# Attention, batch order and routing: a key copy, a product and six operations issued at other places

## The chip, the core and the metric

The kernel runs on one core of one Trainium2 chip. The metric is the device time in microseconds from start to end of one execution; lower is better. The core has five engines with a queue of their own each, and every queue runs strictly in the order in which the program issues: TensorE (PE) multiplies into the PSUM banks, VectorE (DVE) and ScalarE (ACT) read those banks and SBUF, GpSimd (POOL) reads SBUF only, SyncE (SP) issues the loads. Engines wait for each other by semaphores only: an instruction that waits holds up everything behind it on its engine.

## What is computed

Cross attention over 8 batches of 112 tokens, then a feed-forward layer with 8 routed experts (the two best for each token) and a shared one, everything in fp32:

```python
x = x + _L0_xattn_ref(_layernorm(x, axis=-1), ctx_512, L0_xattn_Wq, L0_xattn_Wkv_expand, L0_xattn_Wout)
x = x + _L0_ffn_ref(_layernorm(x, axis=-1), ...)
# attention: 16 heads of 32, causal mask
qp = q @ Wq.T; k, v = jnp.split(latent_kv @ Wkv_expand.T, 2, axis=-1)
out = softmax(mask(qh @ kh.T / sqrt(32))) @ vh          # per head
return out @ Wout.T
# feed-forward
scores = jax.nn.softmax(x @ gate_weight.T, axis=-1)
topk_w, topk_idx = jax.lax.top_k(scores, 2)
act = silu(gu[..., :F]) * gu[..., F:]                   # per expert, F = 352
y = jnp.einsum('tef,te,ehf->th', act, combine, down_weights)
sact = silu(sgu[:, :Fs]) * sgu[:, Fs:]                  # shared expert, Fs = 704
y = y + sact @ shared_down.T
```

## The kernel before

The 896 tokens are 8 batches of 112 rows for the attention and 7 tiles of 128 rows for the rest. Every fp32 operand of a large product is split into a high and a low part ("_hi", made by ScalarE, and "_lo", made by VectorE as the difference), and a product is three passes over the pairs lo-hi, hi-lo, hi-hi. There is no planner: the order on each engine is written out by hand in one block for each engine, and the batches are pipelined across engines.

**Attention, loop over b = 0 to 7.** In iteration b TensorE computes the scores of batch b+1 (`scores`), transposes the four groups r of batch b's probabilities (`transposed(b, r)`), computes the output projection of the batch tile b-2 (`out_proj(b - 2, ...)`, twelve passes into bank D, split 9 and 3 around the last two transposes), transposes tile b-3 of the next layer's input (`t2`), projects the values of batch b+1 (`v_proj`) and multiplies probabilities with values into bank CC (called O(b) here). The key and query projections of the second half of the batches are spread over iterations 0 and 1; the last one, `k_proj(1, 3, CC)`, goes through the same bank CC, so that O(1) has to wait (semaphore KT) until its result is copied out. VectorE does that copy (`put_kT(3)`, helper line L1351) behind `inverse(2, 0)`, `masked(2, 3)`, `inverse(2, 1)`. `inverse(b, r)` takes reciprocals of the row sums and waits for ScalarE's exponentials `exps(b, r)` (L1038); `masked(b, r)` adds the mask and finds the maximum; `put_v` and `oT_lo` follow. GpSimd multiplies the probabilities with the reciprocals (`normalised`, L430) and does the statistics' last step and the normalisation of the next layer (`apply2`). ScalarE copies the transposed probabilities out (`put_pT`, probT) except group 1 of batches 2 and later, which VectorE copies (L1333), and makes `put_x2T` and `put_oT`. From iteration 2 on ScalarE does `put_x2T(b - 3)` before the copies `put_pT(b, 2)` and `put_pT(b, 3)`. `add_attention(n)` (L1298) adds bank D to the residual and takes the statistics.

**Shared stage.** The shared expert's 704 columns are worked off in slices j = 0 to 5; in each, `shared_gu(j, t)` computes gate and up for the token blocks t = 0 (4 tiles) and t = 1 (3 tiles), ScalarE and VectorE make the activation (`shared_silu`, `shared_mul`, L1474, `shared_hi`, `shared_lo`), and `shared_down(j, t)` multiplies with the down weights into four banks, from which VectorE adds into the residual (`add_shared`, L1494). Amid this VectorE does the routing: a chain of small dependent operations, 56 elements wide, each waiting for the one before (`link`): softmax, `pick` (the best expert), `pick` (the second), the sums picked and before, then (semaphore trip) TensorE's rank products (L846 to L849), copies of their result (L1551, L1552) and the slots. GpSimd then scatters the rows to the experts' tiles in memory. In TensorE's order: shared_down(0,0), shared_gu(1,1), shared_down(0,1), shared_gu(2,0), the rank products, shared_down(1,0). `shared_down(0, 1)` waits for the additions of `add_shared(0, 0)` (semaphore sres), since it uses the same banks; `shared_gu(2, 0)` waits for `shared_mul(1, 0)` (sact).

**Expert loop.** 21 tiles of 128 gathered rows, each with its expert's weights split on the fly.

The lines of TensorE's helper `product` are L554, of the transposes L615 (probabilities) and L546 (rows), of the scores L626, of O(b) L763; L993 is ScalarE's helper for the high parts and copies, L1279 VectorE's for the low parts.

Of the kernel before, what the change touches and what calls it, by code (L numbers as in the profile page):

```python
# [43 lines left out]
def build(nc, x, ctxT, wqT, wkvT, woT, gateT, guT, dnT, sguT, sdnT, out):  # L44
# [220 lines left out]
    with nc.Block() as block:  # L265
# [275 lines left out]
        def _(pe):  # L541
# [165 lines left out]
            for b in range(NB):  # L707
# [28 lines left out]
                if b >= 2:  # L736
                    pe.wait_ge(s["QT"], C * NBLK)
                    if b >= 3:
                        pe.wait_ge(s["x1"], b - 2)
                    if b == 2:  # L740
                        pe.wait_ge(s["wo_hi"], C)
                        pe.wait_ge(s["wo_lo"], C)
                    out_proj(b - 2, 0, 9)
                transposed(b, 2)
# [3 lines left out]
                if b >= 2:  # L748
                    out_proj(b - 2, 9, 3 * C)
                if b + 1 < NB:  # L750
# [240 lines left out]
        def _(act):  # L991
# [27 lines left out]
            def put_x2T(n, bank_):  # L1019
                act.wait_ge(s["T2"], n + 1)  # L1020
                hi(x2T[0][:, :, n * P:(n + 1) * P], as_chunks(bank_, P), "x2T_hi")
# [76 lines left out]
            for b in range(NB):  # L1098
# [12 lines left out]
                if b + 1 < NB:  # L1111
                    exps(b + 1, 1)
                if b >= 3:
                    put_x2T(b - 3, CC)
                if b >= 2:
                    put_pT(b, 2)
                    put_pT(b, 3)
# [146 lines left out]
        def _(dve):  # L1264
# [84 lines left out]
            def put_kT(j):  # L1349
                dve.wait_ge(s["K"], C + j + 1)  # L1350
                dve.tensor_copy(kT[1][:, j, :], CC[:, 0:W]).then_inc(s["KT"], 1)  # L1351
# [73 lines left out]
            masked(1, 2)  # L1425
            for b in range(NB):
                if b + 1 < NB:
                    inverse(b + 1, 0)
# [13 lines left out]
                if b >= 2:  # L1442
                    add_attention(b - 2)
                if b == 1:
                    put_kT(3)
                if b + 1 < NB:
# [61 lines left out]
            def pick(p, top, first, oh):  # L1508
# [23 lines left out]

            pick(prb, weight, first1, oh1)
            link(dve.scalar_tensor_tensor(out=prb2[:, :, :], in0=oh1[:, :, :], scalar=-2.0, in1=prb[:, :, :],
                                          op0=ALU.mult, op1=ALU.add))
            pick(prb2, second_w[:, :], first2, oh2)
            link(dve.tensor_tensor(picked[:, 0:NX, :], oh1[:, :, :], oh2[:, :, :], ALU.add))
            for n in range(NX):
# [3 lines left out]
            last.then_inc(s["trip"], 1)  # L1542
            add_shared(0, 0)
            shared_act(1, 0)
            add_shared(0, 1)
# [135 lines left out]
```

## Time and profile before

| | |
|---|---|
| time, median of 3 runs | 344.97 us (343.78 to 345.1) |
| profiled execution | 346.77 us, its span 345.0 us |
| TensorE busy | 327.2 us (95% of the span) |
| VectorE, ScalarE, GpSimd busy | 267.9, 233.1, 133.2 us (78%, 68%, 39%) |
| mean granted TensorE clock | 0.982 of full speed |
| stages in the span | attention to about 108 us, shared stage to about 196, expert loop to the end |

Times in views of the trace are microseconds from the start of the span. Busy TensorE time overstates how full it is, since matmuls are pipelined: one pass of 512 columns is listed with 0.39 us, but the next starts 0.23 us after it. The chain of work that ended last is followed back from the last instruction, at each step to what released it.

### The profile page before, as it was taken

The numbers are of one execution on the slowest core, as the hardware profiler recorded it, in microseconds if no ns is written. First come the engines' busy times: TensorE is split into PE (matmuls) and PEld (weight loads), VectorE is DVE, ScalarE is ACT, GpSimd is POOL, SyncE is SP. The second block draws the span as 40 slices with busy tenths as digits, with TensorE's granted clock in tenths as the row PEclk, the third lists the DMA queues.
The fourth block names the chain that finished last, engine by engine and source line by source line (L and its number), as shares of the span: only waits on it lengthen the run. The fifth ranks groups of instructions, "written<-read, shape, count | busy, mean of one in ns | idle before, by whom it ended". The sixth has DMA issues, their size and how long they took to land.

```text
span 345.0 us, 7024 instructions
## 1 busy us (share of the span) xinstructions
PE 327.2 (95%) x2285; PEld 281.6 (82%) x2285; DVE 267.9 (78%) x675; ACT 233.1 (68%) x582; POOL 133.2 (39%) x144
## 2 busy tenths in 40 slices
PE   7999979999999998999999899999999999999990
PEld 6898858777776786889898778889988998998980
DVE  4889757999936348855487999999998989999930
ACT  4666988999953232312326578898898889889830
POOL 4335464777844000164400007765742321231231
PEclk9999987999999999999999999999999999999996
DMA  7999300000002799994689953564455456455333
GB/s 232 378 341 379 110 1 3 3 2 1 3 2 95 289 357 327 430 327 152 217 253 236 299 179 82 96 135 101 84 117 130 84 89 138 103 89 120 71 42 50
DMA packets 31795, 53.01 MB, mean 154 GB/s; under 512 B 7440, under 2 KB 14992, under 8 KB 30736
## 3 DMA queue, kind: packets, MB, share of 16 engines
q1 hardware_dynamic: 27616, 43.34, 38.4%
q0 software_dynamic: 4144, 9.23, 14.9%
q8 instruction: 19, 0.31, 0.4%
q14 instruction: 16, 0.13, 0.1%
HBM read 32.22 MB, written 16.92 MB: 142 GB/s over the span
## 4 chain that ended last, share of the span: by engine, by line
PE 69%; ACT 10%; DVE 8%; DMA 6%; issue 3%; POOL 2%; POOLq 1%; SPq 0%; DVEq 0%; ACTq 0%
PE bank L554 26%; PE bank L877 21%; ACT prob L1038 5%; PE bank L901 5%; DMA out<-y_sb,dest 3%; PE bank L615 3%; PE bank L905 2%; PE bank L915 2%; PE bank L776 2%; PE bank L763 2%; PE bank L911 2%; DVE gu_parts L1279 2%; PE bank L546 2%; PE bank L626 1%; DMA w_sg<-sguT 1%
## 5 line engine op out<-in xcount | busy, mean ns | idle before, releaser
L533 POOL DMA_INDIRECT out<-y_sb,dest x21 | 38.4, 1830 | 114.9 <-DMA out<-y_sb,dest 68.1
L1279 DVE TENSOR_TENSOR gu_parts<-w_gu,gu_parts 128x704 fp32r<-128x704 f32 x84 | 77.0, 951 | 0.8 <-ACT gu_parts L993 0.4
L993 ACT ACTIVATE gu_parts<-w_gu 128x704 fp32r x84 | 66.2, 793 | 13.9 <-PE bank L877 12.3
L877 PE MATMUL bank<-gu_parts,xsT_hi 128*128 128x352 f32 x328 | 70.0, 335 | 1.4 <-DVE xsT_lo L1279 0.9
L877 PEld LDWEIGHTS bank<-gu_parts,xsT_hi 128*128 128x128 f32 x328 | 53.7, 188 | 8.8 <-issue 8.7
L877 PE MATMUL bank<-gu_parts,xsT_lo 128*128 128x352 f32 x164 | 39.7, 323 | 0.0
L554 PE MATMUL bank<-x2T_hi,w_sg_lo 128*128 128x512 f32 (+1 forms) x88 | 32.7, 372 | 0.2
L430 POOL TENSOR_TENSOR prob<-prob,rrow 112x448 f32<-112x448 f32 x30 | 27.5, 935 | 12.3 <-DVE rrow L1329 12.3
L554 PE MATMUL bank<-x2T_hi,w_sg_hi 128*128 128x512 f32 (+1 forms) x88 | 32.0, 363 | 0.0
L554 PE MATMUL bank<-x2T_lo,w_sg_hi 128*128 128x512 f32 (+1 forms) x88 | 31.9, 363 | 0.0
L506 POOL DMA_INDIRECT xs_dram<-x2n,slot_i x14 | 14.8, 1057 | 37.9 <-DVE eid L1574 33.9
L877 PEld LDWEIGHTS bank<-gu_parts,xsT_lo 128*128 128x128 f32 x164 | 28.7, 189 | 0.0
L993 ACT ACTIVATE act_s_hi<-act_s 128x512 fp32r<-128x512 f32 (+1 forms) x10 | 5.8, 577 | 32.5 <-DVE act_s L1474 18.9
L1279 DVE TENSOR_TENSOR dn_lo<-w_dn,dn_hi 128x1024 fp32r<-128x1024 f32 x21 | 25.6, 1217 | 2.6 <-ACT dn_hi L993 2.6
L1038 ACT ACTIVATE prob<-score,negmax 112x112 f32<-112x112 f32 x64 | 24.2, 405 | 0.0
L993 ACT ACTIVATE dn_hi<-w_dn 128x1024 fp32r x21 | 22.2, 1060 | 2.9 <-PE bank L905 2.9
L1038 ACT ACTIVATE prob<-bank,negmax 112x112 f32<-112x112 f32 x64 | 21.8, 374 | 2.5 <-DVE negmax L1323 2.5
L1494 DVE TENSOR_TENSOR xres<-xres,bank 128x512 f32<-128x512 f32 x35 | 22.3, 680 | 0.4 <-PE bank L807 0.4
L554 PEld LDWEIGHTS bank<-x2T_hi,w_sg_lo 128*128 128x128 f32 x88 | 16.5, 188 | 4.5 <-issue 2.2
L554 PEld LDWEIGHTS bank<-x2T_hi,w_sg_hi 128*128 128x128 f32 x88 | 16.5, 188 | 1.8
L554 PEld LDWEIGHTS bank<-x2T_lo,w_sg_hi 128*128 128x128 f32 x88 | 16.5, 188 | 1.7
L1279 DVE TENSOR_TENSOR w_sg_lo<-w_sg,w_sg_hi 128x1024 fp32r<-128x1024 f32 (+1 forms) x6 | 6.9, 1150 | 13.6 <-ACT w_sg_hi L993 13.6
(216 smaller groups left out, 830.8 us busy)
## 6 DMA issues: line engine op xcount, KB each, us to landing
w_gu<-guT SPq DMA_DIRECT2D x8, 1408.0 KB
xs_dram<-no_row SPq DMA_DIRECT2D x1, 5460.0 KB, 19.6
xs_in<-xs_dram SPq DMA_DIRECT2D x21, 256.0 KB, 4.5
w_dn<-dnT SPq DMA_DIRECT2D x8, 512.0 KB, 5.4
act_w<-act_e SPq DMA_DIRECT2D x19, 176.0 KB, 2.7
w_sg<-sguT SPq DMA_DIRECT2D x10, 256.0 KB, 5.4
w_dn<-dnT SPq DMA_DIRECT2D x8, 192.0 KB, 6.1
w_sd<-sdnT SPq DMA_DIRECT2D x5, 256.0 KB, 6.0
```

The lines of the kernel that those rows point to most:

```text
L430: pool.tensor_tensor(prob[r][:, :, :], prob[r][:, :, :], rrow[:, r, :].unsqueeze(2).to_broadcast([SQ, C, SQ]), ALU.mult)\
L506: pool.indirect_dma_start(out=xs_dram[:, :], out_offset=bass.IndirectOffsetOnAxis(ap=slot_i[:, k, n:n + 1], axis=0), in_=x2n[:, n, :], in_ ...
L533: pool.indirect_dma_start(out=out[:, :], out_offset=bass.IndirectOffsetOnAxis(ap=dest[:, i, 0:1], axis=0), in_=y_sb[i % 2][:, :], in_offse ...
L546: ins = pe.transpose(dst[:, c * P:(c + 1) * P], src[:, c * P:(c + 1) * P], ident[:, :])
L554: ins = pe.matmul(dst, a, b, start=start and n == 0, stop=stop and n == len(passes) - 1)
L615: ins = pe.transpose((A, B)[r % 2][0:SQ, c * SQ:(c + 1) * SQ], prob[r][:, c, :], ident[0:SQ, 0:SQ])
L877: ins = pe.matmul(dst[:, 0:F], xsT[x_][:, c, :], gu2[w_][:, c, f0:f0 + F], start=c == 0 and n == 0, stop=c == C - 1 and n == 2)
L901: pe.matmul(A[:, :], actT_split[0][:, k, :], dn2[part][:, k, :], start=k == 0 and part == 1, stop=False)
L993: act.activation(dst, src, ACT.Copy).then_inc(s[sem], 1)
L1038: ins = act.activation(prob[r][:, c, :], src, ACT.Exp, bias=negmax[:, r, c:c + 1], scale=-1.0, accum_out=rowsum[:, r, c:c + 1])
L1279: dve.tensor_tensor(lo_, src, hi_.bitcast(F32), ALU.subtract).then_inc(s[sem], 1)
L1494: dve.tensor_tensor(xres[:, n, :], xres[:, n, :], (B, CC, D, A)[i][:, :], ALU.add)\
```

## The change

- VectorE: `put_kT(3)` of iteration b = 1 moves from behind `inverse(2, 0)`, `masked(2, 3)`, `inverse(2, 1)` to the front of the iteration.
- TensorE, last iteration b = 7 only: `out_proj(5)` is split 6 and 6 passes instead of 9 and 3 around the transposes `transposed(7, 2)`, `t2(4)`, `transposed(7, 3)`.
- ScalarE, b = 7 only: `put_pT(7, 2)` goes before `put_x2T(4)`; for b = 2 to 6 the order stays as it was.
- VectorE, routing: the four additions `add_shared(0, 0)` and the product `shared_mul(1, 0)` go from behind the sums to behind the first `pick`, and `shared_lo(1, 0)` behind the second `pick` (`shared_act` is these two calls one after the other).

No instruction is added or removed.

```diff
@@ TensorE
+                    early = 9 if b + 1 < NB else 6
-                    out_proj(b - 2, 0, 9)
+                    out_proj(b - 2, 0, early)
                 transposed(b, 2)
                 if b >= 3:
                     t2(b - 3, CC)
                 transposed(b, 3)
                 if b >= 2:
-                    out_proj(b - 2, 9, 3 * C)
+                    out_proj(b - 2, early, 3 * C)
@@ ScalarE
+                if b == NB - 1:
+                    put_pT(b, 2)
                 if b >= 3:
                     put_x2T(b - 3, CC)
+                if 2 <= b < NB - 1:
+                    put_pT(b, 2)
                 if b >= 2:
-                    put_pT(b, 2)
                     put_pT(b, 3)
@@ VectorE, attention
             for b in range(NB):
+                if b == 1:
+                    put_kT(3)
                 if b + 1 < NB:
                     inverse(b + 1, 0)
...
                     add_attention(b - 2)
-                if b == 1:
-                    put_kT(3)
@@ VectorE, routing
             pick(prb, weight, first1, oh1)
+            add_shared(0, 0)
+            shared_mul(1, 0)
             link(dve.scalar_tensor_tensor(out=prb2[:, :, :], in0=oh1[:, :, :], scalar=-2.0, in1=prb[:, :, :],
                                           op0=ALU.mult, op1=ALU.add))
             pick(prb2, second_w[:, :], first2, oh2)
+            shared_lo(1, 0)
             link(dve.tensor_tensor(picked[:, 0:NX, :], oh1[:, :, :], oh2[:, :, :], ALU.add))
...
             last.then_inc(s["trip"], 1)
-            add_shared(0, 0)
-            shared_act(1, 0)
             add_shared(0, 1)
             shared_act(1, 1)
```

## Rows read from the trace of the kernel before

**Rows 1.** The chain that ended last, by engine (part 4 of the page).

```profile
PE 69%; ACT 10%; DVE 8%; DMA 6%; issue 3%; POOL 2%; POOLq 1%; SPq 0%; DVEq 0%; ACTq 0%
```

**Rows 2.** Pieces of that chain, batches 1, 2 and 4: start us, us, what.

```profile
49.33 0.18 DVE rrow L1329
49.51 0.52 DVE kT L1351
...
50.07 1.72 PE bank L763 x32
51.80 1.78 PE bank L626 x32
53.58 1.67 PE bank L615 x8
55.25 2.60 PE bank L554 x9
...
59.36 0.70 DVE xres L1298
...
68.18 0.90 PE bank L763 x32
69.08 0.98 PE bank L626 x32
70.06 0.94 PE bank L615 x8
71.00 2.10 PE bank L554 x9
...
76.21 0.95 PE bank L763 x32
```

**Rows 3.** Engine timelines, batches 1 and 2: start, us, instruction, [idle before <-releaser].

```profile
45.58 0.36 PE L554 MATMUL bank<-ctx_hi,w_kv_hi 128*128 128x448 f32 x1
...
47.75 0.40 PE L554 MATMUL bank<-w_kv_hi,ctx_hi 128*112 128x512 f32 x1
...
46.28 0.08 DVE L1323 DVE_READ_ACCUMULATOR2_ANT negmax<- 112x1 f32 x1
...
56.55 0.59 DVE L1333 COPY probT<-bank 112x448 f32<-112x448 f32 x1
...
51.86 0.54 ACT L1049 ACTIVATE oT_hi<-bank 128x448 fp32r<-128x448 f32 x1 [1.10 <-PE bank L763]
...
45.68 2.53 POOL L452 TENSOR_TENSOR w_o_lo<-w_o,w_o_hi 128x512 fp32r<-128x512 f32 x2
```

**Rows 4.** Busy time of the engines and granted clock (PEclk) in two stretches.

```profile
131.00:132.44 1.44, 0.38 (x3) 0.08 (x2) 1.34 (x6) 0.00 (x0) 0.00 (x0) 1.00 1.01 430
...
49.30:56.20 6.90, 6.13 (x75) 5.41 (x76) 4.58 (x29) 5.15 (x25) 2.80 (x3) 0.51 0.01 2
```

**Rows 5.** Timelines of TensorE and ScalarE before the last batch's product.

```profile
101.47 1.01 PE L763 MATMUL bank<-probT,v_sb 112*32 112x112 f32 x32 [0.47 <-issue]
...
100.43 0.97 ACT L993 ACTIVATE probT<-bank 112x448 f32<-112x448 f32 x2
```

**Rows 6.** Timelines of VectorE and TensorE around the routing, shared stage.

```profile
128.33 0.22 DVE L1514 TENSOR_TENSOR oh<-down,first 128x56 f32<-128x56 f32 x1
...
131.62 2.47 DVE L1494 TENSOR_TENSOR xres<-xres,bank 128x512 f32<-128x512 f32 x4
...
135.45 0.69 DVE L1279 TENSOR_TENSOR act_s_lo<-act_s,act_s_hi 128x512 fp32r<-128x512 f32 x1 [0.76 <-ACT act_s_hi L993]
...
141.88 0.16 DVE L1552 COPY count<-bank 128x8 f32<-128x8 f32 x1
...
132.44 0.47 PE L554 MATMUL bank<-w_sd_hi,act_s_lo 128*128 128x512 f32 x1 [1.07 <-DVE xres L1494]
...
134.84 0.47 PE L554 MATMUL bank<-x2T_hi,w_sg_lo 128*128 128x512 f32 x1
...
140.39 0.33 PE L846 MATMUL bank<-picked,tri 128*128 128x56 f32 x2
```

## The prediction

> **What bounds the kernel now.** I read the chain of work that ended last first, then its pieces in order of time, then the timelines of TensorE, VectorE, ScalarE and GpSimd around the four places that the change touches, and the granted clock last. TensorE carries 69% of the chain [rows 1]. It is dense in most of the span, so the question at each edit is only whether TensorE stands still there, and what it waits for. TensorE stands at three of the touched places. The longest stand is in the second batch (b = 1): TensorE ends the value projection of batch 2 (its last pass runs from 47.75 to 48.15), and the attention product of batch 1, the step O(1), starts 1.92 us later at 50.07, released by VectorE's copy kT at L1351 [rows 2, 3]. After that stand the granted clock is at the lower of its two levels (1.2 instead of 2.4 GHz): its mean is 0.51 between 49.3 and 56.2 [rows 4]. The second is 0.47 us before the last batch's product O(7) at 101.47 [rows 5]. The third is 1.07 us before 132.44, where the down product of the shared stage waits for VectorE's first addition [rows 6].
>
> **Part 1, the key copy (VectorE, b = 1).** The copy's input is there early: the last pass of k_proj(1,3) ends at 45.58 + 0.36 = 45.94 [rows 3]. But the copy stands behind inverse(2,1), which waits for ScalarE's exponentials until 49.33 [rows 2]. In its new place VectorE reaches it when masked(2,2) ends, at 46.36 [rows 3], so the product has been ready for 0.4 us, and the copy ends 0.52 us later, at 46.9. What it is moved past pays: inverse(2,0) and masked(2,3) begin 0.15 to 0.5 us later. The first feeds a product on GpSimd that is queued behind w_o_lo until 45.68 + 2.53 = 48.2 [rows 3], the second is read by ScalarE after 51; both are covered. inverse(2,1) still waits until 49.33 and loses nothing. No DMA is issued between the two places.
>
> Now I walk on from there, each step at its duration at the full clock (product 0.90, scores 0.98, eight transposes 0.94, nine passes 2.10, from batch 4 in [rows 2]):
> - O(1) starts a pass (0.33 us) after 47.75, at 48.08, and ends at 49.0.
> - scores(3) needs the exponentials (2,1), so it waits until 49.35 and ends at 50.35; the transposes of batch 2 end at 51.3.
> - ScalarE stood 1.10 us for O(1) before its copy oT_hi at 51.86 [rows 3]. That goes: it starts at 50.7 and VectorE's oT_lo ends at 51.8. out_proj(0) waits for that and its nine passes end at 53.9 (before: 57.85).
> - The transpose (2,3) needs VectorE's copy probT(2,1). That copy is behind masked(3,0), inverse(2,3), masked(3,1) and masked(3,2), and these now start when oT_lo ends, so it moves only from 56.55 [rows 3] to 54.6 and ends at 55.15. TensorE waits 0.9 us for it.
> - Four transposes and three passes take 1.2 us: out_proj(0) ends at 56.35 where it ended at 59.34 [rows 2].
>
> As a sum: the stand gives 2.0; the lower clock gives (1.72 - 0.90) + (1.78 - 0.98) + (1.67 - 0.94) + (2.60 - 2.10) = 2.85 [rows 2]; three new waits take back 0.35, 0.5 and 0.9. That is 3.0 us. Is it kept? From batch 3 on the batches follow each other at 76.21 - 68.18 = 8.03 us [rows 2] in a loop through all engines (addition, statistics, GpSimd's product, transposes, ScalarE's copy, addition), with no load from memory in it, so a shift of all engines stays. ScalarE is nearly full, and its own shift decides: I walk it to 2.9 us (oT_hi of batch 2). I take **2.9 us**. The unknown is the clock; its other end is 1.15 us (below).
>
> **Part 2, the last batch's order (TensorE and ScalarE, b = 7).** The array is idle from 101.00, so the last pass (0.40 us) had started at 100.60, and O(7) could start 0.33 us behind it, at 100.93. It starts at 101.47, because ScalarE does x2T_hi first and only then, from 100.43 to 101.40, the two probT copies [rows 5]. After the change three passes of out_proj(5) (3 x 0.23) move behind the transposes, so all three transposes come 0.7 us earlier, and one of the two copies runs before x2T_hi. ScalarE is through at 100.25 and VectorE's x2T_lo at 100.5, both before TensorE's passes end, whose number is the same. O(7) starts at 100.93: **0.54 us**. Behind it the statistics of tile 5 hardly move (0.15 us), but t2(5) needs them only 0.3 us or more after they are there. Bounds: 0 (that slack is gone) to 0.54.
>
> **Part 3, the additions amid the routing (VectorE).** The second pick and the running sums stand ahead of the additions at 131.62 [rows 6]. The first pick ends with the row at 128.33, after 0.22 us; the four additions then start at 128.58, and the first ends at 129.27. The array is idle from 132.44 - 1.07 = 131.37, so its last pass of 0.33 us had started at 131.04, and the next could start 0.17 us behind it, at 131.21. So the down product starts there and not at 132.44, and its nine passes of 0.23 end at 133.28. shared_gu(2,0) before had to wait for the product shared_mul(1,0) too (which ends 0.76 us before 135.45, at 134.69) and started at 134.84 [rows 6]; this product now ends at 131.65. Gain at that point 134.84 - 133.28 = **1.56 us**. The bounds are 1.07, the wait alone, and 1.56.
>
> Who pays? The routing is later by four additions (2.39), the product (0.6) and shared_lo (0.6): its sums end at 135.3 where they ended at 131.6. TensorE asks for them at its rank product, at 140.39 before and 138.8 after: 3.5 us of cover. From there VectorE is early: before, it stood 0.76 us for ScalarE's act_s_hi ahead of shared_lo(1,0), and that wait is now filled with the second pick. So the copies rank and count, which ended at 142.04, end at 141.2. TensorE's fourth tile of shared_down(1,0) comes after the rank products (0.6) and nine passes (2.1) from 140.39, at 143.1, and 1.56 earlier is 141.55. This cover is only 0.35 us thin; if it is gone, the excess is lost one for one. SP's weight loads wait on TensorE's counts and move with it. GpSimd's scatter and the loads behind it on SP move by 0.84 us only; I cost that at nothing, because the chain of waits passes through neither in the shared stage, and at up to 0.7 us if they have no slack (second rival).
>
> **Sum.** 2.9 + 0.54 + 1.56 = 5.0 us. The profiled execution took 346.77 us (span 345.0 and 1.77 around it), the change 341.8 by it; the median of the runs shown is 344.97, 1.8 lower, which gives 340.0.
>
> **Rivals.**
> - *The clock falls all the same.* In part 1 TensorE has new pauses of 0.35, 0.5 and 0.9 us. For it: the clock was low after the stand of 1.92 us [rows 2, 4], and the same sort of work surrounds these pauses. Against: the stand of 1.07 us at 131.4 left the clock at 1.00 [rows 4]. If it falls at 51 for as long as before, transposes and nine passes take 1.67 and about 4.2 us, out_proj(0) ends near 58.2, and part 1 is worth 1.15: 344.97 - 3.25 = 341.7. The Trainium skill (TensorE: Matmul & The Clock Gate, section "A second HAM failure mode: psum-queue depth-cycling") says that frequent small pauses between groups of matmuls can make the clock swing between its levels; by that rule this rival holds, and whoever leaves the rule out has the same number from rows 2. This trace has one short stand with the clock kept and one longer with it lost, so it doesn't settle it.
> - *The routing's tail or the start of the expert loop takes over.* rank comes late, or the late expert weights, asked for after the shared stage, don't keep up with the 1.56 us. For it: the cover of 0.35 us. Against: most of the excess has to come from a queue that moves by 0.84 us itself. Price 0.5 to 1.5, in the middle 341.0.
> - *ScalarE absorbs part 1* in the batches, since it is nearly full: part 1 worth 0.5, 342.4.
> - *The copy does not release O(1)*, because another of its waits ends last, or both part 1 and part 3 only trade waits: 342.9 to 344.2.
> - *Slower.* The clock falls in batch 2 and swings on through batches 3 to 6, where every batch lies behind the one before. At the lower level a batch's steps take about 1.8 times as long (1.72, 1.78, 1.67 for 0.90, 0.98, 0.94), so a whole batch of 8.03 us costs some 6 us more. From 0.8 of one batch on the whole gain is gone, from 1.1 on the kernel is measurably slower; at 1.3 batches, 348.
>
> **How the numbers follow.** The forecast 0.58 (its own range 339.0 to 341.0: the three runs shown lie within 1.3 us), clock 0.16, tail 0.10, ScalarE 0.04, traded waits 0.08, slower 0.04. A measurement of this kernel tells about 0.5% (1.7 us) from no change. Below 343.25 lie the forecast, the first three rivals and a part of the fourth: 0.9, less a little for the edges, 0.88; within 0.5% 0.08; slower 0.04. The range runs from 338.9 (part 1 at 3.5, nothing of its waits coming back, and a fast run) to 342.7, which takes in the clock, the tail and ScalarE.
>
> **What would show it.** Right: kT at L1351 starts near 46.4 and O(1) near 48.1; the granted clock is 1.00 from 49 to 56; add_attention(0) starts near 56.4; O(7) has no pause; no wait of TensorE for L1494; shared_gu(2,0) starts 5.0 us earlier than 134.84. Wrong: a stretch of clock below 1 after 49; TensorE waiting for rank (L1551) or for probT beyond 1 us; the expert loop's first gate product less than 5 us earlier than before.

## The result and the profile after

| | before | after |
|---|---|---|
| median of 20 runs, us | 346.11 (343.78 to 349.19) | 344.19 (342.72 to 346.48) |
| ratio | | 0.9947 [0.9928, 0.9966] |
| profiled execution, us | 346.77 (span 345.0) | 346.04 (span 344.2) |
| mean granted clock of that execution | 0.982 | 0.992 |

The kernel became faster, by 1.9 us and not by 5.0; the time lies above the forecast range of 338.9 to 342.7. More runs of before moved its own median up by 1.1 us, to 346.11; that is a part of the distance between 340.0 and 344.19, and the missing 3.1 us of gain are the rest. One execution of e12 (below) took 401.89 us at a mean clock of 0.75 and is left out of that kernel's median. In this document a shift is the time of a mark in a trace minus the time of the same mark in the trace of before; negative is earlier. In the profiled execution of after VectorE's first key copy began 0.30 us later than before's (36.10 and 35.80); "from the start" means with that taken out.

The page of after: busy time by engine, the row of the granted clock in 40 slices, and the chain by engine (compare [rows 1]).

```profile
PE 325.6 (95%) x2285; PEld 280.0 (81%) x2285; DVE 267.3 (78%) x675; ACT 232.9 (68%) x582; POOL 134.3 (39%) x144
...
PEclk9999999999999999999999999999999999999996
...
PE 64%; DMA 11%; ACT 10%; DVE 7%; issue 3%; POOL 1%; SPq 1%; POOLq 1%; DVEq 0%; ACTq 0%
```

TensorE's share of the chain fell from 69% to 64%, and that of DMA rose from 6% to 11%. This points at transfers, and the stages below show which.

**The batches.** TensorE in after, batches 1 and 2: start, us, instruction, [idle before <-releaser]; then VectorE's key copy; then the windows with the granted clock (PEclk, the third number from the end). They answer to [rows 2 to 4]. A line of code after a moved part has shifted by 1 to 5.

```profile
48.04 0.39 PE L554 MATMUL bank<-w_kv_hi,ctx_hi 128*112 128x512 f32 x1
48.36 0.97 PE L764 MATMUL bank<-probT,v_sb 112*32 112x112 f32 x32
49.74 1.05 PE L626 MATMUL bank<-kT,qT 32*112 32x112 f32 x32 [0.40 <-ACT prob L1039]
...
52.30 0.47 PE L554 MATMUL bank<-w_o_hi,oT_lo 128*128 128x512 f32 x1 [0.60 <-DVE oT_lo L1365]
...
55.61 0.57 PE L615 MATMUL bank<-ident,prob 112*112 112x112 f32 x4 [0.64 <-DVE probT L1337]
...
46.57 0.62 DVE L1355 COPY kT<-bank 128x448 f32<-128x448 f32 x1
...
49.00:52.00 3.00, 2.30 (x56) 1.76 (x44) 1.42 (x4) 3.00 (x17) 1.98 (x3) 1.00 0.01 3
52.00:56.00 4.00, 3.06 (x18) 2.49 (x18) 4.00 (x35) 4.00 (x24) 2.15 (x3) 1.00 0.01 2
```

The key copy starts 2.85 us earlier, O(1) follows the value projection without a stand, the three new waits are 0.40, 0.60 and 0.64 us, and the clock stays at the upper level. The addition behind out_proj(0) starts at 56.92 (before 59.36 [rows 2]).

**Last batch and routing.** TensorE in after before O(7) and around the rank product, and VectorE's copy of the counts behind it. They answer to [rows 5, 6].

```profile
98.45 0.78 PE L764 MATMUL bank<-probT,v_sb 112*32 112x112 f32 x24
...
130.21 0.39 PE L554 MATMUL bank<-x2T_hi,w_sg_lo 128*128 128x512 f32 x1
...
135.66 0.33 PE L847 MATMUL bank<-picked,tri 128*128 128x56 f32 x2
...
137.41 0.15 DVE L1557 COPY count<-bank 128x8 f32<-128x8 f32 x1
```

O(7) has no pause, shared_gu(2,0) starts at 130.21 (before 134.84), and the rank product starts at 135.66 right behind a pass, 4.73 us before its place in [rows 6]: 5.03 from the start. Up to here the sum of the prediction holds.

**Weight slice 4 of the shared stage** (j = 4; the name of its load is sg(4), of the down slices' sd). The chain of after from 146 to 161: start us, us, what.

```profile
146.73 0.60 SPq L299
...
147.37 7.45 DMA w_sg<-sguT
...
157.75 0.61 DVE xres L1498
...
158.50 2.30 PE bank L554 x9
```

The same stretch in the timelines of ScalarE, VectorE and TensorE of after; then ScalarE's line and SP's request for the slice in the trace of before; last SP's requests in after for three experts' gate and up weights, ahead of the slice.

```profile
154.83 1.06 ACT L994 ACTIVATE w_sg_hi<-w_sg 128x1024 fp32r<-128x1024 f32 x1 [7.04 <-DMA w_sg<-sguT]
...
155.93 1.23 DVE L1283 TENSOR_TENSOR w_sg_lo<-w_sg,w_sg_hi 128x1024 fp32r<-128x1024 f32 x1 [7.54 <-ACT w_sg_hi L994]
...
158.50 0.47 PE L554 MATMUL bank<-w_sd_hi,act_s_lo 128*128 128x512 f32 x1 [0.66 <-DVE xres L1498]
...
157.86 1.06 ACT L993 ACTIVATE w_sg_hi<-w_sg 128x1024 fp32r<-128x1024 f32 x1 [5.61 <-DMA w_sg<-sguT]
...
151.46 1.38 SPq L299 DMA_DIRECT2D w_sg<-sguT  x2
...
130.78 1.39 SPq L319 DMA_DIRECT2D w_gu<-guT  x3
```

SP asks for the two halves of slice 4 from 146.73 on, 4.73 us earlier than before (151.46). But the slice is there only at 154.83, 3.03 us earlier than before (157.86). ScalarE reaches the split of this slice and stands 7.04 us (before 5.61, without a pause of TensorE behind it); VectorE stands behind ScalarE, and the additions of shared_down are queued behind VectorE's w_sg_lo and w_sd_lo. So TensorE gets a pause of 0.66 us at 158.50, and the first pass behind its nine (160.89) starts 0.25 us later than in the rhythm of the passes, behind the product that VectorE forms after the additions. Before had neither. From 120 to 150 the 16 DMA engines are full; the windows of after and of before (last three numbers: PEclk, DMA share, GB/s):

```profile
120.00:150.00 30.00, 30.00 (x153) 26.52 (x153) 23.46 (x63) 9.14 (x14) 7.04 (x7) 1.00 1.00 381
...
120.00:150.00 30.00, 28.84 (x146) 25.00 (x147) 21.91 (x61) 9.64 (x15) 3.94 (x4) 1.00 0.96 361
```

**The expert loop.** The transposes of the first gathered tile start at 178.15 (before 181.64, shift -3.49), the first gate product at 187.45 (190.97), those of the last tile at 320.24 (322.25, shift -2.01), and the span is 0.8 us shorter. The chain of after and then of before for what is lost on the way:

```profile
234.53 4.14 DMA act_w<-act_e
...
288.36 4.26 DMA act_w<-act_e
...
308.88 4.25 DMA act_w<-act_e
...
325.08 6.26 DMA out<-y_sb,dest
...
332.09 4.95 DMA out<-y_sb,dest
...
327.09 5.43 DMA out<-y_sb,dest
...
333.27 4.68 DMA out<-y_sb,dest
```

Each tile sends its activations through a copy from SBUF to SBUF (act_w<-act_e, 176 KB). Its median is 2.8 us; three of the 19 took over 4 us in this execution, and TensorE waited for each of them. From request to the next transposes a tile takes some 3.8 us in any case, so each of the three cost 0.3 to 0.5 us (an estimate: 4.18, 4.31 and 4.29 for 3.8). The last two scatters took 11.21 us together against 10.11 before.

### The profile page after: what moved, and what is told of

Read it like the earlier page. It is cut to its first block, busy times and chain, and to the rows that moved or that the text cites. A ratio compares the mean times of both kernels' runs of the same rounds, so it can differ in the third digit from the quotient of the medians.

```text
span 344.2 us, 7026 instructions
## 1 busy us (share of the span) xinstructions
PE 325.6 (95%) x2285; PEld 280.0 (81%) x2285; DVE 267.3 (78%) x675; ACT 232.9 (68%) x582; POOL 134.3 (39%) x144
## 4 chain that ended last, share of the span: by engine, by line
PE 64%; DMA 11%; ACT 10%; DVE 7%; issue 3%; POOL 1%; SPq 1%; POOLq 1%; DVEq 0%; ACTq 0%
PE bank L554 25%; PE bank L878 19%; ACT prob L1039 5%; PE bank L902 4%; DMA act_w<-act_e 4%; DMA out<-y_sb,dest 3%; DMA w_sg<-sguT 2%; PE bank L615 2%; PE bank L916 2%; PE bank L906 2%; PE bank L777 2%; DVE gu_parts L1283 2%; DMA w_kv<-wkvT 2%; PE bank L912 1%; PE bank L546 1%
## 5 line engine op out<-in xcount | busy, mean ns | idle before, releaser
L533 POOL DMA_INDIRECT out<-y_sb,dest x21 | 40.0, 1906 | 116.6 <-ACT y_sb L1211 63.8
L1283 DVE TENSOR_TENSOR gu_parts<-w_gu,gu_parts 128x704 fp32r<-128x704 f32 x84 | 76.1, 939 | 0.8 <-ACT gu_parts L994 0.7
```

Of the source, the lines that this page charges most:

```text
L533: pool.indirect_dma_start(out=out[:, :], out_offset=bass.IndirectOffsetOnAxis(ap=dest[:, i, 0:1], axis=0), in_=y_sb[i % 2][:, :], in_offse ...
L1283: dve.tensor_tensor(lo_, src, hi_.bitcast(F32), ALU.subtract).then_inc(s[sem], 1)
```

## The experiments

Two questions were open: where between the rank product and the end the 5.0 us went, and how much of the 5.0 us a typical execution of before pays at all, since the largest term rests on a fall of the clock seen in one execution. The shifts against the trace of before, in us; "start" is the offset with which the profiled execution began (VectorE's first key copy), and belongs to every number of its row. T(0), T(2) and T(20) are the transposes of the first, third and last gathered tile.

| kernel | start | O(2) | rank product | T(0) | T(2) | T(20) | span | median of runs, us | ratio to before, 95% |
|---|---|---|---|---|---|---|---|---|---|
| after | +0.30 | -2.46 | -4.73 | -3.49 | -3.33 | -2.01 | -0.8 | 344.19 | 0.9947 [0.9928, 0.9966] |
| e8, after again | +0.12 | -2.64 | -4.86 | -3.40 | -2.96 | -3.34 | -3.4 | 343.74 | 0.9943 [0.9912, 0.9974] |
| e1, parts 1 and 2 | +0.14 | -2.61 | -3.75 | -3.14 | -2.78 | -1.86 | -2.0 | 344.74 | 0.9943 [0.9915, 0.9970] |
| e2, part 3 | +0.17 | +0.13 | -1.61 | -0.38 | -0.03 | +0.85 | +1.7 | 346.69 | 1.0018 [0.9989, 1.0046] |
| e3, part 1 | +0.05 | -2.69 | -3.59 | -3.13 | -1.26 | -1.69 | -1.9 | 344.64 | 0.9961 [0.9935, 0.9986] |
| e4, first load order | +0.17 | -2.60 | -4.88 | -1.19 | +1.05 | +0.42 | +0.4 | 348.44 | 1.0075 [1.0046, 1.0104] |
| e5, second load order | -0.09 | -2.85 | -4.99 | -4.97 | -3.40 | -2.73 | -2.4 | 344.14 | 0.9930 [0.9897, 0.9962] |
| e6, before + that order | +0.02 | -1.30 | -1.52 | -1.52 | -1.14 | +0.02 | +1.0 | 346.94 | 0.9995 [0.9966, 1.0025] |
| e7, before, stand filled | +0.19 | -2.04 | -3.01 | -1.82 | -1.48 | -2.19 | -1.8 | 344.66 | 0.9944 [0.9915, 0.9973] |
| e9, after, late loop | +0.11 | -2.66 | -4.97 | -0.11 | -0.11 | -0.26 | -0.3 | 346.61 | 1.0033 [1.0007, 1.0060] |
| e10, e5 + late store | +0.15 | -2.61 | -4.76 | -4.77 | -5.41 | -5.53 | -5.7 | 342.60 | 0.9908 [0.9875, 0.9941] |
| e11, after + late store | +0.29 | -2.47 | -4.76 | -4.12 | -4.47 | -4.40 | -4.1 | 342.34 | 0.9854 [0.9807, 0.9901] |
| e12, before + both | +0.04 | -1.27 | -2.14 | -2.05 | -2.48 | -1.42 | -0.9 | 345.28 | 0.9956 [0.9925, 0.9987] |

Kernels of one group ran on one chip, with before beside them: e1 to e4 (median of before 346.12), e5 to e7 (346.93), e8 to e10 (346.12, another chip), e11 and e12 (346.35). The ratio is not the quotient of the two medians; the two agree within 0.2% but for e11, where the medians give 0.9884 and the ratio 0.9854.

**e1_parts12: parts 1 and 2, without part 3.** From after, the routing's additions are put back:

```diff
             pick(prb, weight, first1, oh1)
-            add_shared(0, 0)
-            shared_mul(1, 0)
...
             pick(prb2, second_w[:, :], first2, oh2)
-            shared_lo(1, 0)
...
             last.then_inc(s["trip"], 1)
+            add_shared(0, 0)
+            shared_act(1, 0)
             add_shared(0, 1)
```

> Parts 1 and 2 of the change (key copy, last batch's order), the routing as before. In the changed kernel the shift against before is 3.0 us behind the last batch, 4.7 after the rank products and 3.5 at the first gate product of the expert loop. Theory A (a load takes part 3 back: the fourth shared weight slice lands when the chain of weight loads that starts with out_proj(6) lets it): this kernel reaches the loop 3.3 to 3.5 us earlier than before, like the changed kernel, and its time is within 0.4 us of the changed one. Rival B (part 3 carries its 1.5 us into the loop and the rest is lost by chance later): it reaches the loop 1.5 us later than the changed kernel and takes 1.5 us more.

The rank product came 3.75 us earlier and the expert loop 3.14. After with part 3 has 4.73 and 3.49. So part 3 brings about 1.0 us (1.14 from the start) to the rank product and 0.35 (0.51) to the loop; in the ratios nothing of it is seen (0.9943 here without it, 0.9947 and, in e8, 0.9943 with it). Neither theory is met in full: theory A wanted 3.3 to 3.5 us at the loop (3.14) and a time within 0.4 us of after's (344.74, 0.55 above), and rival B's 1.5 us is far from both.

**e2_part3: part 3 alone, in the kernel before.**

```diff
             pick(prb, weight, first1, oh1)
+            add_shared(0, 0)
+            shared_mul(1, 0)
...
             pick(prb2, second_w[:, :], first2, oh2)
+            shared_lo(1, 0)
...
-            add_shared(0, 0)
-            shared_act(1, 0)
             add_shared(0, 1)
```

> Part 3 alone (the additions amid the routing), attention as before. Theory A: TensorE gains 1.6 us at the rank products and has given back all but 0.2 to 0.5 us at the first gate product; time 0 to 0.5 us below before. Rival B: 1.5 us at both places and in the time.

At the rank product part 3 gives 1.78 us from the start, at the loop 0.55, and in the median nothing that can be told from zero. The mechanism of part 3 is right at its place, and the gain does not survive the shared stage, with parts 1 and 2 or without. From the rank product to the loop e2 loses 1.23 us, as after does (1.24), and its trace has the pause behind slice 4 too:

```profile
161.59 0.47 PE L554 MATMUL bank<-w_sd_hi,act_s_lo 128*128 128x512 f32 x1 [0.62 <-DVE xres L1494]
```

**e3_part1: part 1 alone.**

```diff
             for b in range(NB):
+                if b == 1:
+                    put_kT(3)
                 if b + 1 < NB:
...
-                if b == 1:
-                    put_kT(3)
                 if b + 1 < NB:
                     put_v(b + 1)
```

> Part 1 alone (key copy first on VectorE in batch 1). Both theories: product of batch 2 starts 2.4 to 2.9 us earlier, granted clock 1.00 from 49 to 56, the shift is the same at the last batch and behind it; the loop starts 2.5 to 2.9 us earlier. If the expert loop keeps what reaches it, the time falls by 2.5 to 2.9 us; if the loop gives part of it back (rival C: its own chain of scatters and copies through memory), by 1 to 2 us.

The loop starts as early as in e1 (-3.13 and -3.14), so part 2's half microsecond is nearly gone by then too. Part 1 alone carries the start of the loop. The three terms also overlap at the rank product. TensorE's wait for the first addition, 1.07 us in [rows 6], is 0.57 in e1 and 0.23 in e3:

```profile
128.70 0.47 PE L554 MATMUL bank<-w_sd_hi,act_s_lo 128*128 128x512 f32 x1 [0.57 <-DVE xres L1498]
...
128.84 0.47 PE L554 MATMUL bank<-w_sd_hi,act_s_lo 128*128 128x512 f32 x1 [0.23 <-DVE xres L1494]
```

So parts 1 and 2 already shorten the stand that part 3 removes; part 3 is worth 1.70 us behind O(7) alone (e2) and 1.14 on top of parts 1 and 2. In e1 VectorE reaches the additions 3.75 us earlier than in before (127.87 for 131.62), TensorE ends its passes only 3.24 us earlier; why VectorE gains more wasn't followed up. The median, 344.64, is near the 344.74 of e1 and 1.5 us below before: what is seen in the medians, part 1 gives. In this execution another 1.9 us were lost at the third gathered tile; TensorE in e3, and the windows around it:

```profile
194.41 0.88 PE L877 MATMUL bank<-gu_parts,xsT_hi 128*128 128x352 f32 x4 [1.12 <-DVE xsT_lo L1279]
...
196.27 1.22 PE L877 MATMUL bank<-gu_parts,xsT_hi 128*128 128x352 f32 x3 [0.65 <-issue]
...
194.00:198.00 4.00, 2.94 (x12) 2.70 (x13) 4.00 (x5) 1.27 (x2) 0.00 (x0) 0.77 0.69 216
```

Two pauses of 1.12 and 0.65 us, and the clock was below its upper level with them.

**e4_loads: after, with slices 4 ahead of the last expert weights on SP.** If slice 4 comes late because it is queued behind 1.4 MB loads of expert weights, it must come in time when SP asks for it first.

```diff
-            for e in range(5, E):
+            for e in range(5, E - 1):
                 load_gu(e, s["wegu"])
+            next_sd(5)
+            next_sg(4)
+            next_sd(4)
+            load_gu(E - 1, s["wegu"])
             for e in range(n_early):
                 load_dn(e, s["wedn"])
-            next_sd(5)
-            next_sg(4)
-            next_sd(4)
             next_sg(5)
```

> The changed kernel with SyncE's order altered: the fourth slice of the shared weights and the down slices are asked for before the last expert's gate weights and before the early down weights, so that less data stands ahead of them. Theory A: the slice lands 3 us or more before ScalarE wants it, ScalarE's wait of 7.0 us for it shrinks to under 3, TensorE's two pauses near 158.5 and 160.8 (0.7 and 0.6 us) are gone, and the first gate product comes 1.2 us earlier than in the changed kernel; time 1.2 us lower if the loop keeps it. Rival B: the slice is late for another reason (its request, not the data ahead), the pauses stay and nothing changes.

Slice 4 was split at 151.69 and the pauses at 158 were gone. But next_sd(4) waits on SP for a buffer that comes free only at 159.80, and everything behind it is asked for after that. The chain of e4:

```profile
159.80 0.33 SPq L305
...
162.28 10.24 DMA w_sg<-sguT
...
175.24 2.32 PE bank L555 x9
```

Slice 5 lands at 172.5 and TensorE stands 3.12 us before 175.24. The kernel was slower than before. The point for slice 4 is made; the edit was a bad one, since one wait on an in-order queue held the last expert's gate and up weights, the early down weights and slice 5.

**e5_slice_first: the same with next_sd(4) left where it was**, behind the last expert weights. The order on SP is then gu(5), gu(6), sd(5), sg(4), gu(7), the early down weights, sd(4), sg(5).

```diff
             next_sd(5)
             next_sg(4)
-            next_sd(4)
             load_gu(E - 1, s["wegu"])
             for e in range(n_early):
                 load_dn(e, s["wedn"])
+            next_sd(4)
             next_sg(5)
```

> The changed kernel, and on SyncE only the fourth slice of the shared weights (with the down slice before it) is asked for ahead of the last expert's gate weights and the early down weights; the down slice that waits longest stays behind them. Theory A (the slice was late for the data ahead of it): it lands about 3 us earlier, both pauses of TensorE near 158.5 are gone, the fifth slice is not late, the first gate product comes 1.2 us earlier than in the changed kernel, near 186.2, and the time falls by 1 us or a little less. Rival: another transfer is late in its place and the loop starts no earlier.

ScalarE's split of slice 4 in e5:

```profile
152.21 1.06 ACT L995 ACTIVATE w_sg_hi<-w_sg 128x1024 fp32r<-128x1024 f32 x1 [4.12 <-DMA w_sg<-sguT]
```

No pause of TensorE is left between 140 and 190. The shift of -4.99 at the rank product is -4.97 at the first gathered tile, and the first gate product starts at 186.14 where 186.2 was expected. This shows the cause of the first loss (1.24 us in after): slice 4 behind the expert weights. The size of the loss varies between executions of the same code: 1.46 us in e8, 0.64 in e11. Yet the median was 344.14 and the shift at the third tile -3.40. The chain of e5 there:

```profile
191.49 6.03 DMA act_w<-act_e
```

This copy took 6.03 us where its median is 2.8; SP had asked at 188.85 for the store of the first five tiles' sums (out<-xres, 1.28 MB). In after the same store stands as far ahead of the same copy, but there the copy took 3.8 us and TensorE didn't wait for it.

**e6_slice_first_old: the kernel before with e5's load order.** The diff is e5's.

> The kernel before with the same order of loads, and nothing else of the change. Theory A: TensorE had no pause for the slice there, so the first gate product comes within 0.3 us of before's 190.97 and the time is that of before within 0.5 us. Rival (the load order is worth something by itself): 1 us less.

The load order does nothing for the kernel before: the ratio is 0.9995, so slice 4 was no bound there. But the first gate product starts at 189.42, 1.55 us earlier than before's and not within 0.3 of it. Its trace showed something else. Everything up to O(2) is the code of before, and still O(2) came 1.30 us earlier than in the trace of before. The windows of e6:

```profile
50.00:52.00 2.00, 1.92 (x48) 1.59 (x52) 0.66 (x3) 1.47 (x7) 0.52 (x1) 0.68 0.02 4
52.00:54.00 2.00, 2.00 (x30) 1.80 (x25) 1.61 (x12) 1.33 (x9) 0.93 (x1) 0.50 0.00 0
54.00:56.00 2.00, 2.00 (x12) 1.73 (x11) 1.85 (x20) 2.00 (x11) 0.93 (x1) 0.97 0.02 4
```

The clock fell later and came back earlier than in [rows 4], for some 3.4 us and not 6.9 (each window's share below 1, over the 0.5 between the levels). e12 shows the same windows, e2 the long fall.

**e7_fill_stand: the kernel before, TensorE's stand filled.** Before its wait for the key copy TensorE waits for a count that it has reached anyway and does 14 transposes of the identity that nobody reads. No useful work is moved; only the array is kept busy.

```diff
+                if b == 1:
+                    pe.wait_ge(s["QT"], C * NBLK)
+                    for _ in range(14):
+                        pe.transpose(D[:, 0:P], ident[:, :], ident[:, :])
                 pe.wait_ge(s["KT"], C + 3 if b == 0 else C * NBLK)
```

> The kernel before, with 14 transposes (of no use to the result, into bank D, which is free) in TensorE's stand ahead of O(1) in batch 1; the copy kT stays late. Theory D (in the kernel before the clock falls behind that stand in about two executions of three only, since the mean clocks of its runs lie in two groups, up to 0.988 and from 0.990 on, so the median gains less by part 1 than the profiled execution): here the clock stays at 1.00, O(1) starts at 50.1, O(2) comes 1.0 to 1.8 us earlier than 59.95, all mean clocks are 0.990 or above, and the median is 0.7 to 1.2 us below before. Rival: the clock is not what costs the time behind the stand, O(2) stays near 59.9 and the time is that of before.

TensorE in e7, and its windows:

```profile
48.19 1.75 PE L756 MATMUL bank<-ident 128*128 128x128 f32 x14
50.26 0.97 PE L767 MATMUL bank<-probT,v_sb 112*32 112x112 f32 x32 [0.32 <-DVE kT L1355]
...
49.00:52.00 3.00, 2.68 (x73) 2.27 (x71) 1.32 (x4) 2.65 (x14) 1.22 (x2) 1.00 0.01 3
52.00:56.00 4.00, 3.62 (x33) 2.84 (x26) 4.00 (x33) 4.00 (x24) 2.42 (x3) 1.00 0.01 2
```

O(1) starts as late as in before (50.26 and 50.07, the start being 0.19 later), the clock stays at the upper level, and O(2) comes 2.04 us earlier. The median fell by 2.3 us (ratio 0.9944), more than the 0.7 to 1.2 expected, and the mean clocks of its executions lie between 0.991 and 0.994. So the clock was a true cost of the stand, and keeping it up is worth about as much as the whole change. The two groups of mean clocks that the expectation speaks of weren't there in more executions of before: 9 of 98 have 0.989.

**e8_changed_again and e9_late_loop: after once more, and after with the loop held back.** e8 is after unchanged. In e9 TensorE does 31 useless transposes ahead of the last slice's products, so that the loop starts 3.3 us later and all before it stays as it is:

```diff
+            pe.wait_ge(s["sact"], NBLK * (ND - 1) + 1)
+            for _ in range(31):
+                pe.transpose(S[0][:, 0:P], ident[:, :], ident[:, :])
             shared_gu(ND, 0)
```

> The changed kernel once more, to stand on the same chip as the next two. Its loop reaches tile 0 about 3.5 us earlier than the profiled execution of before, its median is 1.5 to 2.5 us below before. Theory C (the expert loop and its start give a part back, because the copy of the activations through memory is slow in some tiles): a loss of 0.5 to 2 us between the first and the last gathered tile, at other tiles than last time. Theory D (before is a mixture of executions with and without the fall of the clock, and the loop gives nothing back on average): the loss is within 0.5 us of zero.

> The changed kernel with 31 transposes (about 3.4 us of TensorE, of no use to the result) ahead of the last slice of the shared stage, which puts the loop back to where it began in before. Theory D (the loop takes the same time whenever it begins): the median is 3.2 to 3.5 us above the changed kernel's. Theory C (an earlier loop meets unfinished transfers and loses what it gained): the loads have time to finish, and the median rises by only 1 to 2.5 us.

3.3 us at the loop start are 2.87 us in the median (346.61 - 343.74), between the 3.2 to 3.5 of theory D and the 1 to 2.5 of theory C: what comes to the loop is mostly kept. In e9 the loop starts where the trace of before starts it (-0.11), and its median is still 0.5 above that of before on the same chip (1.1 us by the ratio, interval 0.2 to 2.1). That fits a typical execution of before reaching the loop 0.5 to 1.1 us earlier than the profiled one did; it is argued, not shown, since it takes the loop's own time to be the same in both. e8 has at T(20) and the end what it had at the loop (-3.40, -3.34, -3.4), while after's own profiled execution lost 1.5 and then 1.2 us. The last two scatters in e8:

```profile
323.75 5.24 DMA out<-y_sb,dest
...
329.74 4.54 DMA out<-y_sb,dest
```

They took 9.78 us, against 11.21 in after's trace for the same code, and beyond the copy behind the store e8 has no copy of over 4 us on its chain, where after has three. The same kernel spreads by that much from one execution to the next.

**e10_store_late: e5, with the store moved behind the activation copy.**

```diff
-            sp.wait_ge(s["sres"], NX * ND - XB[1] + 1)
-            start_sum(0, BLK + 1)
             sp.wait_ge(s["Tx"], 2)
...
             sp.wait_ge(s["eact"], 1)
             act_words()
+            sp.wait_ge(s["sres"], NX * ND - XB[1] + 1)
+            start_sum(0, BLK + 1)
```

> The kernel of e5 (slice of the shared weights asked for earlier), and on SyncE the 1.28 MB store of the residual goes behind the first copy of the activations, which took 6.0 us behind it in e5 and held TensorE back at the second tile. Theory C: that copy takes 3 to 4.5 us, the shift of 4.8 us at gathered tile 1 is still above 4.2 at tile 2 (e5: 3.4), and the median is 0.5 to 1.2 us below the changed kernel's. Rival: the copy is slow for the late expert weights, not for the store, and nothing changes.

The order on SP in e10 and in e5 (start, us, the request):

```profile
191.71 0.82 SPq L386 DMA_DIRECT2D act_w<-act_e  x1
192.57 4.08 SPq L379 DMA_DIRECT2D out<-xres  x2
...
188.85 0.39 SPq L379 DMA_DIRECT2D out<-xres  x1
191.49 0.55 SPq L388 DMA_DIRECT2D act_w<-act_e  x1
```

The first two copies take 2.5 and 2.9 us, the shift at the third tile is -5.41, at the end -5.7, and the median 342.60, 1.1 us below e8's on the same chip. The loss at the start of the loop is shown: the copy stood behind the store. The edit also puts the load of the third tile's rows (xs_in) ahead of the store; that load took 6.7 us in e5 and 3.2 in e10. The chain of e5 ends with the copy, but the two weren't tried one by one.

**e11_store_only and e12_old_both: after with the late store alone, and the kernel before with the load order and the late store.** Their diffs are those of e10 and e5.

> The changed kernel with the late store alone (the slice of the shared weights asked for as in the changed kernel). If both brakes are separate: the shift at gathered tile 0 is that of the changed kernel (3.4 to 3.5 us against before), it is kept or grows by up to 0.6 us at tile 2, where e5 lost 1.4; the median is 0.3 to 1 us below the changed kernel's and about 1 us above e10's (342.6).

> The kernel before with both edits of SyncE's order (slice asked for earlier, store later), none of the change. Together with e10 it measures what the three parts of the change are worth once nothing in the load queue takes them back: by the walk 5.0 us, less 0.5 to 0.8 for the executions of before in which the clock doesn't fall, so e10 should be 3.8 to 4.5 us below this kernel. This kernel itself: 0 to 1 us below before. Rival (the two edits are what made e10 fast, not the change): it lies within 1.5 us of e10.

e11 was as fast as e10 (342.34 and 342.60, on two chips; the intervals of the ratios overlap). The microsecond between them that the load order should be worth is 0.65 us in the two traces at T(0), -4.12 and -4.77, and isn't seen in the medians. At T(0) 3.4 to 3.5 us were expected of e11: in this execution slice 4 was there a little earlier than in after (154.83) and e8 (154.86), and TensorE had no pause behind it. ScalarE's split of slice 4 in e11:

```profile
154.23 1.06 ACT L994 ACTIVATE w_sg_hi<-w_sg 128x1024 fp32r<-128x1024 f32 x1 [6.00 <-DMA w_sg<-sguT]
```

e12 gained 1.1 us on before. Between e12 and e11, on one chip, lie 2.9 us; by the ratios of e10 and e12 the change is worth 0.48% or 1.7 us with both edits in place. The 1.7 is near the 1.5 of the rival, the 2.9 lies between it and the 3.8 to 4.5 of the theory: neither is confirmed in full.

## Why the prediction was wrong

**Right: the mechanism of each part, and the size of the sum up to the rank product.**

| from the start, us | forecast | measured |
|---|---|---|
| O(1) starts | 48.08 | 48.06 |
| three new waits | 0.35, 0.5, 0.9 | 0.40, 0.60, 0.64 |
| add_attention(0) starts | 56.35 | 56.62 |
| part 1, at O(2) | 2.9 | 2.76 |
| part 2, between O(2) and O(7) | 0.54 | 0.56 |
| part 3, between O(7) and the rank product | 1.56 | 1.71 |
| sum | 5.0 | 5.03 |

That the sum is right to 0.03 us is in part luck. The working added the parts as if each gained the same alone and with the others. But of the 1.71 us between O(7) and the rank product 0.56 come in e1 as well, which has no part 3, since parts 1 and 2 shorten the same stand; on top of them part 3 gives 1.14 us where 1.56 were forecast.

The rival of the clock that falls all the same is refuted: it is 1.00 in every window from 46 to 60 of after, and the mean clock of the changed kernel's executions lies between 0.987 and 0.995. The Trainium skill says that frequent small pauses between groups of matmuls can make the clock swing (TensorE: Matmul & The Clock Gate, section "A second HAM failure mode: psum-queue depth-cycling"). After's trace doesn't show it: pauses of 0.40, 0.60 and 0.64 us within 7 us left the clock at 1.00; in e3 pauses of 1.12 and 0.65 us did go with a lower one (0.77). The cover for the routing's tail held: no wait for rank, and the copies of rank and count moved by 4.47, more than the 3.98 that the working gave (0.84 and the 3.44 of parts 1 and 2, less the start of 0.30). ScalarE did not absorb part 1.

**The first step that failed** reads "SP's weight loads wait on TensorE's counts and move with it." The requests did move, by 4.73 us; the landing moved by 3.03. I had costed a request where the transfer sets the time, and a queue in which three loads of expert weights of 1408 KB each stand ahead, at a DMA share of 0.96 (the window of before above). The lateness reached TensorE in steps that the working did not contain: ScalarE's in-order wait for the slice held VectorE's split behind it, and that held the additions, for which TensorE waited. e5 removes the cause: the loop starts 4.97 us earlier instead of 3.49. The second rival had the right size for it (0.5 to 1.5) and named the late expert weights, but as the victims of the lead; they were what stood in its way. On top of part 1, parts 2 and 3 bring 1.39 us to the rank product and 0.61 to the loop (after against e3, from the start).

**The second step that failed** is the term of 2.85 us for the lower clock. In the profiled execution it is about right (the nearest measure is e7, which keeps the clock up and moves nothing: O(2) comes 2.23 us earlier from the start), and it was counted in full for the median. In 98 executions of before beside the experiments the mean clock ran from 0.979 to 0.995; 22 had 0.990 or more, and 19 had 0.984 or less as the profiled one (0.982). Those 22 took 1.2 us less than the others. In e6 and e12 (profiled executions of other kernels whose code up to O(2) is that of before) the fall is about half as long, and O(2) comes 1.3 us earlier. So part 1 is worth less in the median than 2.9. By how much isn't settled: e9 says 0.5 us less at the loop (1.1 by its ratio), the trace of e6 1.3 less, e7 hardly less. The mean clocks speak for 1.3: their median is 0.987 in these 98 executions and 0.992 in the 20 of after, and 0.005 of 345 us, over the 0.5 between the levels, is 3.4 us at the lower level (an estimate), as long as the fall in e6.

**The third point** is smaller. At the loop start the lead meets the store of 1.28 MB, in front of the activation copy (3.8 us in after, 4.88 in e8, 6.03 in e5; 2.5 and 2.2 in e10 and e11, where the store comes later). Before has the store in front too, and there the copy took 4.4 us and TensorE didn't wait for it. The prediction said nothing about the expert loop but that it would be 5 us earlier.

Together, for the median: 5.0, less 1.24 for slice 4, times 2.87/3.3 for what the loop passes on, less 0.5 for the clock, gives 2.8, and with 1.3 in place of 0.5 it gives 2.0. Measured are 1.9 (1.2 to 2.5) and, in e8, 2.0 by its ratio (0.9 to 3.0) or 2.4 by the medians. So the second term may account for all that is missing, but this split is argued and not shown: slow copies and scatters spread by as much. Nor is it settled why e10 isn't faster than e11.

The chances: I gave 0.88 to faster by over 0.5%; the ratio is 0.9947, at the very edge of it. The range was too narrow since all its cases took for granted that every execution of before pays the full fall of the clock and that the loads flow, the two points at which one trace can't speak for the median and TensorE's rows can't speak for a transfer.

**The best version** is after with the late store, with or without e5's load order: 342.34 us (ratio 0.9854 [0.9807, 0.9901]) and 342.60 (0.9908 [0.9875, 0.9941]). Both beat before. Against after, e10 is 1.1 us faster than e8 by the medians on one chip (the intervals of the ratios overlap); e11's interval lies wholly below after's, but was measured on another chip and in six executions.

## What to carry to other kernels

Where an engine becomes earlier, look at each transfer that it will need next, not at when it is asked for but at what is queued in front of it and how full the DMA engines are there; then at which in-order engine will stand for it and what is queued behind that wait. Before a lower clock in one trace is priced, compare the mean clocks of many executions: take the length of the fall that is typical, not the one in the profile. A kernel that comes earlier at a large store should be tried with the store behind the small copy that the next product needs.

## What the runs showed of the hardware

- The same code had a fall of the granted clock of different length after the same stand of 1.9 us: from 49.4 to 56.2 in the profiled execution of before, some 3.4 us (an estimate from the windows), beginning between 50 and 52, in e6 and e12. The mean clocks of 98 executions of before ran from 0.979 to 0.995.
- 14 useless transposes (1.75 us of work) in that stand kept the clock at its upper level and made the kernel 0.56% faster (0.27 to 0.85) with nothing else changed.
- A copy of 176 KB from SBUF to SBUF, 2.8 us in the median, took 3.8 to 6.0 us in eleven traces in which it was asked for some 2.6 us after a store of 1.28 MB, and 2.5, 2.2 and 3.8 us in e10, e11 and e12, in which the store came behind it. Among the other copies, none to three of an execution took over 4 us on the chain: three in after and none in e8, the same code. The one near 288 took 4.26 us in after, e1 and e5 alike; why wasn't followed up.
- The last two scatters of the same kernel took 11.21 us in one execution and 9.78 in another.
